# One program for the first layer and the experts, and a fourth attention unit that gets its bias from GpSimd

## The reference

```python
x = L0_attn_x
xn = _layernorm(x, axis=-1)
s = _L0_attn_ref(xn, ...)          # 16 heads of 8, a relative position bias is added to the scores
g = _silu(_L0_ffn_ref(xn, ...))    # 8 experts, each token goes to its best 2
x = x + s * g
xn = _layernorm(x, axis=-1)
s = _L1_attn_ref(xn, ...)          # causal, three gains
g = _silu(_L1_ffn_ref(xn, ...))    # a linear layer with a low-rank correction
x = x + s * g
```

## Time and profile before

| | |
|---|---|
| median of 3 runs | 951.52 us (950.36 to 954.12) |
| the profiled execution | 959.06 us, of which the span from the first to the last instruction is 957.2 us |
| busy | PE 748.8 us (78%), DVE 647.3 us (68%), ACT 530.0 us (55%), POOL 440.2 us (46%) |
| mean granted clock of TensorE | 0.908 of full speed |

### The profile page before, as it was taken

One profiled execution on the slowest core, in us unless ns is written; L12 is line 12 of the kernel. 1 busy time (PEld: TensorE's weight loads), 2 busy tenths in 40 slices (PEclk: granted clock), 3 DMA queues, 4 the chain that ended last, 5 costly groups with the idle time before them and its releaser, 6 DMA issues. The chain is left out here.

```text
span 957.2 us, 20662 instructions
## 1 busy us (share of the span) xinstructions
PE 748.8 (78%) x6321; PEld 510.7 (53%) x6323; DVE 647.3 (68%) x1142; ACT 530.0 (55%) x924; POOL 440.2 (46%) x550
## 2 busy tenths in 40 slices
PE   0786478799999999962888888525579999999982
PEld 0552244455655655531777777414456666766651
DVE  6634488489888889861666666567257777778741
ACT  2234235377777777670666666548446656566450
POOL 8001777465664664440355455465132343443323
PEclk9997698799999999985899999857689999999995
DMA  5549845344644645215122112150547767767421
GB/s 147 200 78 146 201 120 136 94 107 114 141 108 111 143 106 116 47 44 171 49 60 60 56 58 61 63 148 20 116 101 146 158 156 154 163 156 158 109 58 48
DMA packets 132371, 105.97 MB, mean 111 GB/s; under 512 B 23285, under 2 KB 124345, under 8 KB 129241
## 3 DMA queue, kind: packets, MB, share of 16 engines
q1 hardware_dynamic: 122076, 91.10, 42.0%
q0 software_dynamic: 4320, 8.92, 2.8%
q10 hardware_dynamic: 5920, 5.24, 1.7%
HBM read 54.54 MB, written 49.90 MB: 109 GB/s over the span
## 5 line engine op out<-in xcount | busy, mean ns | idle before, releaser
L1351 DVE TENSOR_REDUCE mx<-ps 128x4 f32<-128x1024 f32 (+1 forms) x224 | 267.8, 1217 | 95.7 <-PE ps L1596 45.7
L1502 ACT ACTIVATE probs<-probs 128x1024 f32<-128x1024 f32 x128 | 131.9, 1053 | 74.6 <-DVE probs L1361 64.7
L1644 PE MATMUL ps<-probs,vpad 128*32 128x256 f32 (+1 forms) x2048 | 125.7, 371 | 7.9 <-ACT probs L1502 7.5
L1510 ACT ACTIVATE probs<-ps 128x1024 f32<-128x1024 f32 x96 | 96.3, 1022 | 58.4 <-DVE ps L1392 58.2
L1265 POOL TENSOR_TENSOR probs<-probs,tabB 128x1024 f32<-128x1024 f32 x42 | 99.4, 2367 | 56.9 <-ACT probs L1517 56.9
L1622 PE MATMUL ps<-qs,ks 99*128 99x256 bf16 x768 | 115.6, 277 | 5.7 <-DMA qs<-mT 3.4
L748 DVE TENSOR_SCALAR probs<-ps,gub 128x128 f32<-128x128 f32 x284 | 80.0, 344 | 54.4 <-PE ps L688 50.5
L1594 PE MATMUL ps<-tabA,eyeb 128*128 128x512 bf16 x256 | 101.7, 397 | 17.3 <-DMA ks<-parts_d 10.7
L1361 DVE TENSOR_TENSOR probs<-ps,tabB 128x1024 f32<-128x1024 f32 x86 | 100.7, 1217 | 13.5 <-PE ps L1622 13.5
L1596 PE MATMUL ps<-ks,qs 96*128 96x256 bf16 x512 | 101.9, 281 | 0.0
L1622 PEld LDWEIGHTS ps<-qs,ks 99*128 99x128 bf16 x768 | 67.9, 98 | 47.9 <-issue 25.4
(11 more groups left out here) (226 smaller groups left out, 1369.5 us busy)
## 6 DMA issues: line engine op xcount, KB each, us to landing
parts_d<-qk SPq DMA_DIRECT2D x64, 192.0 KB, 3.8
qs<-parts_d SPq DMA_DIRECT2D x32, 384.0 KB, 4.9
ks<-parts_d SPq DMA_DIRECT2D x32, 384.0 KB, 6.7
parts_d<-qk SPq DMA_DIRECT2D x64, 128.0 KB, 2.4
od_d<-ev SPq DMA_DIRECT2D x64, 128.0 KB
slots_in<-probs SPq DMA_DIRECT2D x1, 4615.0 KB
probs<-slots_in SPq DMA_DIRECT2D x71, 65.0 KB, 1.8
parts_d<-qk SPq DMA_DIRECT2D x64, 64.0 KB, 1.9
```

The source lines that it names most:

```text
L1351: nc.vector.tensor_reduce(mx[:, s.buf(), t, heads[0]:heads[-1] + 1], ring[:, slot].rearrange("p (h n) -> p h n", n=w), AX.X, ALU.max).then ...
L1502: nc.scalar.activation(probs[:, j, :], probs[:, j, :], ACT.Exp).then_inc(exp_done, 1)
L1510: nc.scalar.activation(probs[:, j, :], ring[:, slot], ACT.Exp).then_inc(exp_done, 1)
L1644: mm = nc.tensor.matmul(od[32 * q:32 * q + 32, T * (i % 2) + t0:T * (i % 2) + T], vpad[:, b, 4 * c + q, at:at + 32], probs[:, j, w * n:w * ...
```

## The change

The program after has two blocks, setup and the rest. `attention(nc, v, 0)` no longer opens a block but returns its five instruction streams, and `experts` calls each of them ahead of its own stream. What used to be steps 17 and 18 is spread: the last products with v and one store stand at the seam, and the two last divisions stand between the bodies of the first tiles of the experts (`between`, called with k = -1 to 6). The experts' weights are loaded in three pieces, after steps 14 and 15. The second products of the experts use other PSUM banks, because `od` and `misc` (banks 6 and 7) are still in use. On TensorE the reading of `owner` is moved from the head of a body to behind the first products. Unit B5 joins `ASIDE`. The parts of the expert biases are made of 9 rows instead of 41, without the wait for `small_mm`.

```diff
-BIASES = 5 * E + 1
+BIASES = E + 1
...
-        attention(nc, v, 0)
-        attention(nc, v, 1, middle(nc, v, experts(nc, v)))
+        first = attention(nc, v, 0)
+        second = attention(nc, v, 1, middle(nc, v, experts(nc, v, first)))
+        with nc.Block() as block:
+            block.sync(second[0])
...
             dve.wait_ge(eb_load, 48)
             for c in range(PARTS):
-                nc.vector.tensor_copy(b3[:, c, :], braw[:]).then_inc(eb_parts, 1)
+                nc.vector.tensor_copy(b3[:, c, :], blast).then_inc(eb_parts, 1)
                 if c < PARTS - 1:
-                    if c == 0:
-                        dve.wait_ge(small_mm, 1)
                     dve.wait_ge(eb_parts, 2 * c + 2)
...
         def body(s):
 
-            if s.has(-2):
-                e2 = owner(pe, nc.tensor, held, s, -2)
             if s.has(1):
...
             if s.has(-2):
+                e2 = owner(pe, nc.tensor, held, s, -2)
                 b = s.buf(-2) % 2
                 pe.wait_ge(a_done, s.n(-2) + 1)
...
-        run(pe, body)
+        before[4](pe)
+        pe.wait_ge(v.w_load, 48)
+        pe.wait_ge(v.b_load, 16)
+        run(pe, body, before[5].tensor)
...
-    ASIDE = () if layer else (0, 2, 3)
-    ORDER = tuple(range(NU)) if layer else (1, 0, 2, 4, 5, 6, 3, 7)
+    ASIDE = () if layer else (0, 2, 3, 5)
+    ORDER = tuple(range(NU)) if layer else (1, 0, 2, 4, 3, 6, 7, 5)
...
     SEQ = ((("take", 0),), (("exp", 1),), (("take", 2), ("exp", 0)), (("take", 3), ("exp", 2)), (("exp", 4),),
-           (("exp", 5),), (("exp", 6), ("exp", 3)), (("exp", 7),))
+           (("take", 5), ("exp", 3)), (("exp", 6),), (("exp", 7), ("exp", 5)))
...
-        pipeline(eng, body, -1 if layer else -2, LOOP, 3, B - 1 - DIV, 3, B)
+        pipeline(eng, body, -1 if layer else -2, LOOP, 3, B - 1 - DIV if layer else B, 3, B)
...
+            def division(k):
+                if k == 6:
+                    sums_in(last)
+                    outputs_in(last)
+                    inverses_out(last)
+                    inverses_in(last)
...
+            def division(k):
+                if k == 0:
+                    scale(last)
+                if k == 1:
+                    project(last)
+                if k == 3:
+                    invert(last)
+                if k == 6:
+                    scale(drained)
+                    project(drained)
...
+            for i in range(2, NU):
+                values(last, -2, i)
+
+            def division(k):
+                if k == 0:
+                    outputs(last)
+                if k == 6:
+                    outputs(drained)
```

More of the change, by code:

```diff
@@ L604, in pipeline, with experts @@
         body(Step(k, 0, period, count))
-def experts(nc, v):
+def experts(nc, v, before):
     sem = v.sem
@@ L638, in experts, with run @@
     row_done, weighed = sem("ex_rows"), sem("ex_weights_out")
[L640 to L641 removed]
+    def run(eng, body, between=None):
+        pipeline(eng, body, -1, 7, 7, SLOT_TILES + 2, FLIGHT, SLOT_TILES, between)
     def owner(eng, ns, held, s, d):
@@ L662, in body @@
                 sp.dma_start(xg[:, b, :], v.slots_in[bass.ds(s.n(1) * P, P), :]).then_inc(x_load[b], 16)
-        run(sp, body)
+        before[0](sp)
+        run(sp, body, before[5].sync)
         for b in range(4):
@@ L762, in body @@
                                         ).then_inc(row_done, 1)
-        run(dve, body)
+        before[2](dve)
+        run(dve, body, before[5].vector)
     def gpsimd(pool):
@@ new lines, in store, with body @@
+        def store(s):
+            act.wait_ge(fin_done, s.n(DIV) + 1)
+            act.dma_start(v.out[bass.ds(s.n(DIV), 1)].rearrange("b (c p) d -> p (b c) d", p=P),
+                         yt[:].rearrange("p (c d) -> p c d", c=2)).then_inc(out_st, 16)
+        def body(s):
+            if layer == 0 and s.k < HELP and s.has():
+                if s.has(-1):
+                    act.wait_ge(v_full, s.n(-1) + 1)
+                nc.scalar.activation(xb[:], xnT[:, bass.ds(s.n() * T, T)], ACT.Copy).then_inc(xb_done, 1)
+            for pos, (kind, j) in enumerate(U.order):
+                if pos == A_PART and s.has(2):
+                    parts_one(s)
+                if pos == A_OUT and s.has(-2):
+                    outputs(s)
+                if kind == "B" and U.exists(s.k, kind):
+                    for what, i in (SEQ[j] if apart(s.k) else (("exp", j),)):
+                        if what == "take":
+                            take(s, i, U.slot(s.k, pos))
+                        else:
+                            exponential(s, i, U.slot(s.k, pos))
+                if pos == A_TWO and s.has(2):
+                    parts_two(s)
+                if pos == A_VAL and s.has():
+                    values(s)
+                if pos == A_MAX and s.has():
+                    max_rows(s)
+            if layer and s.has(DIV):
+                store(s)
+            if layer == 0 and s.k in (B - 2, B - 1):
+                act.wait_ge(full["B"], NU * s.k)
+                half = slice(0, E // 2) if s.k == B - 2 else slice(E // 2, E)
+                act.dma_start(v.wgu[:, half], v.gu_w[half].rearrange("e h n -> h e n")).then_inc(v.w_load, 16)
+                if s.k == B - 1:
+                    act.dma_start(v.wdn, v.down_w.rearrange("e (c i) h -> i e c h", c=2)).then_inc(v.w_load, 16)
+            if A_MAX >= len(U.order) and s.has():
+                max_rows(s)
```

1000 lines of the change are left out of this document (491 added, 509 removed).

## The result

The changed kernel takes 946.27 us (median of 11 runs, 941.74 to 949.25), the kernel before 953.85 us in as many runs of the same measurement (949.91 to 957.34). The ratio is 0.9925, with a 95% interval of 0.9902 to 0.9948: 0.75% faster, some 7 us. Forecast were 2.0% and 932.5 us, in a range of 917 to 949. The sign and the range held; the gain is under half of the forecast.

A forecast was written before the change was run, and what follows sets the result against it. TensorE was taken to bound the first layer's steady part, not VectorE; in the experts it is busy 140.58 of 160.91 us. Terms sum to -19.0 against 959.06; that 2.0% on the 951.52 median gives 932.5 us, range 917 to 949.

The forecast's parts named there:

- Setup: Before the first layer: without VectorE's wait routing starts sooner and the block opens at 82.6, -7.4 us.
- The fourth unit: First layer's steps 4 to 15: ScalarE's copy frees B5's slot later, A0 begins 1.05 us later, +12.6 us.
- The clock: First layer's steps: longer TensorE pauses bring a half-speed stretch, 1.65 us each, in two of twelve steps, +3.4 us.
- the first rival: First layer: the clock falls in nearly every step; 948.9 us at 1.65 a step, 968 at 3.25; chance 0.11.
- The seam: Between first layer and experts: first tile turned at 438.4 plus 0.5 instead of 452.99, -14.1 us.
- the 4 to 5 that were named: Sign at the seam: 4 to 5 us from last store's issue to first transpose, instead of 18.4.
- The divisions: Moved into the experts' first tiles: TensorE waits 3.0 us with k = 0 and 2.3 with k = 6, +5.3 us.
- The moved reading: Experts' tiles: reading of `owner` hidden behind the first products, 0.285 us less a tile over 66 tiles, -18.8 us.
- The rival that it only moves: Experts' tiles: second products start later by what the transpose gains, -18.8 falls away, 951.3 us; chance 0.12.

The follow-up runs named there:

- before_setup: The kernel before, with the expert biases split from 9 rows and without the wait for TensorE's turned rows, nothing else; 942.28 us, 0.9891.
- warm: The changed kernel with two throwaway TensorE products ahead of A0 in each step from 4 on; 926.82 us, 0.9739 of before.
- three_units: The changed kernel with the fourth unit taken back, order of exponentials as before, the rest kept; 917.61 us, 0.9639 of before.
- joined_only: The changed kernel with three units, the reading ahead of the transpose and VectorE's setup wait restored; 943.51 us, 0.9909 of before.
- scale_sooner: The changed kernel with B5's copy ahead of B4's exponential, divisions sooner, and VectorE's second scaling after tile 5; 909.03 us, 0.9543 of before.
- before_reading: The kernel before, with TensorE's reading of the expert's number behind the first products, nothing else; 937.33 us, 0.9811.
- reading_between: The kernel before, with that reading between the transpose and the first products; 953.85 us, 1.0011.
- before_four: The kernel before, with the fourth unit as in the change and nothing else of it; 980.39 us, 1.0284.

## Why the prediction was half right

- **Setup, -7.4; measured -10.4** (`before_setup`). The chain was right, down to the zeroing at 48.4 and the block 0.3 behind ScalarE. Too small was ScalarE's end, 2.7 sooner instead of 5.96: the sum counted the wait of 2.84 and not the low clock that followed it, 2.96 us more. The base of 90.00 was a late one (87.5 to 89.6 in three other runs), so that against them the block opens 8.3 to 10.4 us sooner.
- **The fourth unit, +12.6; measured +12 to 13.** A0 starts 1.03 us later against the maxima copy, and the steps with the clock at 1.00 are 19.00 - 17.92 = 1.08 longer (`warm` against `three_units`), 11.9 us over the twelve.
- **The clock, +3.4; measured +18.** This is the step that failed: the number of steps in which the clock falls. "I put it at two of twelve steps" was twelve of twelve, 20.49 - 19.00 = 1.49 us each, the first rival with its price per step (1.65) nearly exact; its 948.9 us is close to the 946.3 measured. The price came from rows, the count did not. The rows behind this list show why the early steps could not give it.
- **The seam, -14.1; measured -13.4** (`joined_only`), and 4.35 us from store to transpose, in the 4 to 5 that were named.
- **The divisions, +5.3; measured +4.7.** The one part, 3.0 for tile 0, is 5.75 - 2.67 = 3.1 from the second transpose to the third; the other came to 1.6 instead of 2.3. Not seen was that nearly all of it can be saved: the first division fits in the five microseconds for which TensorE stands at the seam, and the second costs no wait when its reciprocal and its scaling come sooner (`scale_sooner`: the first eight tiles in 15.7 us, 15.3 in `before_reading`).
- **The moved reading, -18.8; measured -18** (`before_reading`, interval 16 to 20; 15.7 by the medians, 16.6 by the trace from the first transpose to the last). By the trace it is 0.24 to 0.26 us a tile. The rival that it only moves is what `reading_between` shows, for another place.

The count rested on the early steps. The reason given for it, pauses "a bit shorter" than those of the early steps, was a true reading (1.08, 0.38 and 0.61 us ahead of 143.4 before, 0.66 and 1.17 in the change) and settled nothing. Between the first two maxima copies a product of the first pass waits for 1.12 us, in the kernel before and in the change. The products right behind it run at full speed in the one trace and at half speed in the other, where the granted clock is 0.50 from 125.2 to 128.4:

```profile
136.74 0.39 PE L1594 MATMUL ps<-tabA,eyeb 128*128 128x512 bf16 x1 [1.12 <-DVE probs L1361]
136.97 0.38 PE L1596 MATMUL ps<-ks,qs 96*128 96x256 bf16 x2
```

```profile
125.03 0.47 PE L1632 MATMUL ps<-tabA,eyeb 128*128 128x512 bf16 x1 [1.12 <-DVE probs L1383]
125.29 0.64 PE L1634 MATMUL ps<-ks,qs 96*128 96x256 bf16 x2
```

Eight of the twelve traces reach this pause at full clock; five of them have the slow stretch right behind it, three have not. The steady part is all or nothing: the slow stretch is in twelve of twelve steps in the two kernels that have the pair of pauses (the change and `before_four`), and in none of the twelve in the ten others. Why it comes every time there is not shown. That 946.3 us still lies in the range is partly luck: without the 3 us that setup gave beyond its term it would have been at the edge.

The measured parts that were run alone give -10.4 + 27.1 - 8.7 - 18.0 = -10.0 against the -7.2 of the whole; the intervals of the four and of the whole are 2 to 2.5 us wide to each side. Almost all of what the forecast missed is the clock's 15 us, part of it given back by the 3 us in setup, which are the clock as well. The remaining 1.8 us behind the tiles and the 3.0 in the first three steps of the table are within what executions of one kernel differ by.

## What to carry to other kernels

When an edit makes TensorE wait once more per iteration of a steady loop, price the wait and, from the rows of the same trace, the slow stretch that may follow it, and work out both cases, the stretch in every iteration and in none; here it was one or the other in all twelve traces, never two steps in twelve. A pause removed can give the same back, as in setup. Relieving an engine that is 89% busy was worth nothing by itself here: look at which instruction frees the buffer that the bounding engine waits for, and put that one first on its engine (here the copy ahead of an exponential turned a loss of 27 us into a gain of 3). And the read into a register on TensorE's sequencer was free behind the sixteen queued instructions of the first products and cost some 0.24 us a tile at both other places.

## What was not expected of the hardware

In the changed kernel a step ends with a pause of 0.66 us ahead of the turn of the maxima and, 1.1 us of work later, one of 1.17 us; 3.2 us at the 1.2 GHz level follow in every step. In the kernel before the first of the two is the same, 0.2 us are left of the second (0.84 in all), and none follow. The Trainium skill (TensorE: Matmul & The Clock Gate, Part 1, the table of its two levels) gives the low level to an array that is idle; the trace has those two levels, and here the low one came to an array that was 91% busy over these steps. Filling the pause with products that nobody reads made the kernel 2% faster. And the steps with the slow stretch settled on one length, 20.48 to 20.49 us, in both kernels that have it, whatever the first ones were (20.55 and 20.61). Why just this length is left open.
